# Two-layer graph network: layer 1's 17 coefficients in three column groups of the array in place of four

## The chip, the cores and the metric

The kernel runs on one core of a Trainium2 chip. The metric is the device time of one execution in microseconds (us). The core has a matrix engine (PE, with its weight loads shown apart as PEld), a vector engine (DVE), a scalar engine (ACT), GpSimd (POOL) and a queue that only issues transfers (SP). PE's clock is granted at one of two levels, 2.4 GHz (shown as 1.0) or 1.2 GHz (0.5).

## The reference, cut to what matters

```python
edge_index = jnp.stack([src, dst])                     # 200000 edges, sorted by dst; 12500 nodes of 32 features
h = jnp.maximum(_layernorm(x, axis=-1), 0.0)
x = x + _L0_gnn_ref(h, edge_index, edge_weight1, edge_attr_3, edge_attr_5, L0_gnn_W)
h = jnp.maximum(_layernorm(x, axis=-1), 0.0)
x = x + _L1_gnn_ref(h, ...)
# layer 1, per edge: x = h[src], y = h[dst], c = w_comp[etype] (16 numbers)
    msg = sum over b of c[b] * (x @ weight[b])          # 16 matrices of 32 x 32
    a = tanh(relu(sum(x_hat * y_hat) / sqrt(32)))       # x_hat, y_hat: linear in x, y and the edge type
    nei = segment_sum(a * msg, dst)
    curr = h[src of the node's last edge] @ self_loop_weight
    h_new = relu(nei + curr), 0 for nodes without edges
```

Layer 0 has the same shape, with 9 coefficients per edge and fixed combinations of small matrices.

## The kernel before, in words

The edges are cut into tiles of 128, twelve tiles to a group (J = 12), 131 groups for each layer. For a group, DVE writes Z: for every edge the layer's coefficients times a one-hot row over the 14 nodes that the tile can touch (WN = 14).
```python
def gather(g):
    wait(pool, L.summed, g.order() - 4)
```

Of the kernel before, what the change touches and what calls it, by code (L numbers as in the profile page):

```python
# [39 lines left out]
ACT = mybir.ActivationFunctionType  # L40
AX_X = mybir.AxisListType.X

N, F = 12500, 32
E = 200000
NREL, NBASE = 86, 16
P = 128
# [26 lines left out]
MQ = P // F  # L73
# [4 lines left out]
C0, C1 = 9, 17  # L78
PASSES = -(-N // WN)

QS = [[0, 3, 6, 9, 9], [0, 5, 9, 13, 17]]
CQ = [3, 5]
NQ = [3, 4]
NOWHERE = NWIN + 1
EPS = 1e-5

# [78 lines left out]
def wait(eng, sem, n):  # L165

    if not isinstance(n, int) or n > 0:
        eng.wait_ge(sem, n)
# [28 lines left out]
def build(nc, x, src_t, dst_t, dnext_t, dst, etype, edge, tile_first, tile_last, group_first, group_last, group_of_tile,  # L197
# [8 lines left out]
    with ExitStack() as ctx:  # L206
        def sb(name, shape, dt=F32):
            return ctx.enter_context(nc.sbuf_tensor(name, shape, dt))
# [28 lines left out]
        eps = sb("eps", [P, 1])  # L237
        cg_sb = sb("cg_sb", [P, CQ[0], F])
        w0_sb = sb("w0_sb", [P, CQ[0], F])
        w0c = sb("w0c", [P, CQ[0], 2 * F])  # L240
        w0_sum = sb("w0_sum", [P, CQ[0]])
        w1_sb = sb("w1_sb", [P, CQ[1], F])
        a1b_sb = sb("a1b_sb", [F, KA])
# [67 lines left out]
        flat = p_left[:].rearrange("p m k -> p (m k)")  # L311
        at = 2 * CQ[1] * HW
        G_sb = flat[:, 0:at].rearrange("p (c h w) -> p c h w", c=CQ[1], h=2)
# [279 lines left out]
        def _(pe):  # L593
# [29 lines left out]
            def edge_sums(n):  # L623
                L = layers[n]
                qs, cq = QS[n], CQ[n]
                no = OUT[n].stop - OUT[n].start
# [25 lines left out]
                def project(g):  # L652

                    hh, w = g.halves()

                    pe.wait_ge(L.G_set, g.order())
                    wait(pe, L.o_set, g.order() - 1)
                    wait(pe, L.added, g.order() - 1)
                    for h in range(hh):
                        for c in range(cq):  # L660
                            rows = NQ[n] * F
                            last = pe.matmul(o_ps[0:w, h, 0:no], G_sb[0:rows, c, h, 0:w], weights[0:rows, c, :],  # L662
                                             start=(c == 0), stop=(c == cq - 1))
                    last.then_inc(L.turned, 1)

                def project_in_quarters(g):

                    hh, w = g.halves()

                    pe.wait_ge(L.G_set, g.order())  # L670
                    wait(pe, L.oT_set, g.order() - 1)
                    wait(pe, L.added, g.order() - 1)
                    for c in range(cq):
                        rows, q = (P, c) if c < MQ else (F, 0)
                        last = pe.matmul(oT_ps[q * F:(q + 1) * F, 0:hh * w], weights[0:rows, c, :], G_sb[0:rows, c, 0:hh, 0:w],  # L675
                                         start=(c < MQ), stop=(c > 0), tile_position=(0, q * F))
                    last.then_inc(L.projected, 1)

                def sum_quarters(g):
# [10 lines left out]
                def place_rows(g):  # L690

                    hh, w = g.halves()

                    pe.wait_ge(L.o_set, g.order())
                    pe.wait_ge(L.R_set, g.order())
                    wait(pe, L.added, g.order() - 1)
                    pe.nop().then_inc(L.turn_go, 1)
                    for h in range(hh):
                        last = pe.matmul(win_ps[OUT[n]], o_sb[0:w, h, 0:no], R[0:w, g.b, h, :], start=(h == 0),  # L699
                                         stop=(h == hh - 1), tile_position=(0, OUT[n].start))  # L700
                    last.then_inc(L.placed, 1)

                def sum_edges(g, back):

                    wait(pe, L.G_set, g.order() - 1)
                    pe.wait_ge(L.gathered[g.q], g.gathers(n) * 16)
                    if not g.tail:
                        pe.wait_ge(L.picked, g.tiles_before(n, 1))
                    pe.wait_ge(L.Z_set, g.order() * 2 - 1)  # L710
                    for j in range(g.nj):
                        if j == JH:

                            pe.wait_ge(L.Z_set, g.order() * 2)
                        bank = G_ps[:, j // JH, 0:cq * HW].rearrange("p (c j n) -> p c j n", c=cq, j=JH)
                        for q in range(NQ[n]):
                            last = pe.matmul(bank[q * F:(q + 1) * F, 0:qs[q + 1] - qs[q], j % JH, :], xg[:, g.q, j, :],  # L717
                                             Z[:, g.b, j, qs[q] * WN:qs[q + 1] * WN], start=True, stop=True,
                                             tile_position=(0, q * F))
                        if j == g.nj - 1:  # L720
                            last.then_inc(L.summed, 1)
                        if back and j == min(g.nj, J // 3) - 1:
                            place_rows(back)

                def step(gs):
                    tiles = gs[0].found_tiles(n) if gs[0] else []
                    find_rows(tiles[0:1])
                    if n == 0 and gs[2]:
                        project(gs[2])
                    if n == 1 and gs[2]:  # L730
                        project_in_quarters(gs[2])
                    find_rows(tiles[1:])
                    if n == 1 and gs[2]:
                        sum_quarters(gs[2])
                    if n == 1 and gs[0]:
                        attention_rows(gs[0])
                    if gs[1]:
                        sum_edges(gs[1], gs[2])
                    elif gs[2]:
                        place_rows(gs[2])  # L740
# [49 lines left out]
        def _(act):  # L790
# [34 lines left out]
            def edge_copies(n):  # L825
                L = layers[n]
                cq = CQ[n]
# [42 lines left out]
                def copy_G(g):  # L870
                    hh, w = g.halves()

                    act.wait_ge(L.summed, g.order())
                    wait(act, L.turned, g.order() - 1)
                    bank = G_ps[:, 0:hh, 0:cq * HW].rearrange("p h (c w) -> p h c w", c=cq)
                    to = G_sb[:, 0:cq, 0:hh, 0:w].rearrange("p c h w -> p h c w")
                    if n == 1:
                        act.activation(to[0:F, :, cq - 1, :], bank[0:F, :, cq - 1, 0:w], ACT.Copy)  # L878
                    chunks, rows = min(cq, MQ), NQ[n] * F
                    act.activation(to[0:rows, :, 0:chunks, :], bank[0:rows, :, 0:chunks, 0:w], ACT.Copy).then_inc(L.G_set, 1)  # L880

                def copy_oT(g):
                    hh, w = g.halves()
# [11 lines left out]
                def step(gs):  # L895
                    if gs[2]:
                        copy_G(gs[2])
                    if n == 1 and gs[0]:
                        one_hots(gs[0])
                    if n == 1 and gs[2]:  # L900
                        copy_oT(gs[2])
                    if n == 1 and gs[1]:
                        attention(gs[1])
                    if n == 1 and gs[0]:
                        last_edges(gs[0])
                    if gs[1]:
                        placing(gs[1])
                    if gs[2]:
                        copy_o(gs[2])
# [439 lines left out]
def _quarters(w, layer):  # L1349
# [3 lines left out]
    for q in range(4):  # L1353
        lo, hi = QS[layer][q:q + 2]
        to[q, :, 0:hi - lo] = w[lo:hi].transpose(1, 0, 2)
# [58 lines left out]
```

## Time and profile before

| | |
|---|---|
| median of 3 runs | 4632.38 us (4622.65 to 4634.9) |
| the profiled execution | 4637.38 us |
| its span, first to last instruction | 4635.5 us |
| PE busy | 3578.4 us (77%) |
| DVE busy | 2689.9 us (58%) |
| POOL busy | 2301.7 us (50%) |
| ACT busy | 1097.0 us (24%) |
| mean granted clock of PE | 0.851 |

Layer 0 fills about the first 2130 us of the span, layer 1 runs from about 2220 us to the end. Busy time of PE counts matmuls by their recorded starts and modelled ends. Whether an engine sets the time is read from who waits for whom in a step, not from its share.

### The profile page before, as it was taken

To read this page: it belongs to the slowest core of one execution; us is meant where nothing else is said; L and a number is where in the kernel's file an instruction comes from. 1 tells how busy PE (TensorE), PEld (TensorE's weight loads), DVE (VectorE), ACT (ScalarE), POOL (GpSimd) and SP (SyncE) were. 2 spreads that over 40 slices of the span, in tenths; PEclk is the share of its full clock that TensorE was granted. 3 is DMA by queue.
4 is the path that set the end of the run, shared out by engine and by line. 5 is a ranking of instruction groups with operands and counts; after the bars stand their busy time and mean duration, and the time that the engine had idled before them with its cause. 6 is when DMAs were issued, how large, how long until landed. Compare 5 with 4: busy or idle time off the path is not lost.

```text
span 4635.5 us, 106735 instructions
## 1 busy us (share of the span) xinstructions
PE 3578.4 (77%) x41254; PEld 3052.1 (66%) x41254; DVE 2689.9 (58%) x3863; ACT 1097.0 (24%) x2563; POOL 2301.7 (50%) x2427
## 2 busy tenths in 40 slices
PE   3788888888888888885677777777777777777777
PEld 2677777777777777775566666666666666666666
DVE  5455555555555555555555665656656665556565
ACT  1111111111111111112233333333333333333332
POOL 5555555555555555553344444544444444445442
PEclk9889988888988989997788888888888888888887
DMA  3111111111111111111122222222222222222221
GB/s 102 21 21 20 20 21 19 20 20 21 20 20 21 20 20 21 21 20 54 35 38 39 38 37 38 40 37 37 37 41 37 38 39 38 37 37 39 39 37 35
DMA packets 216608, 150.09 MB, mean 32 GB/s; under 512 B 121048, under 2 KB 197261, under 8 KB 216079
## 3 DMA queue, kind: packets, MB, share of 16 engines
q0 software_dynamic: 77504, 39.84, 8.9%
q1 hardware_dynamic: 137999, 100.77, 8.8%
q8 instruction: 335, 5.49, 0.5%
q10 hardware_dynamic: 576, 2.40, 0.1%
q14 instruction: 194, 1.59, 0.1%
HBM read 134.58 MB, written 8.22 MB: 31 GB/s over the span
## 4 chain that ended last, share of the span: by engine, by line
PE 38%; issue 13%; another core or an unknown queue 2%; DVE 1%; ACT 1%; ACTq 0%; DVEq 0%
PE ps L636 20%; PE ps L717 7%; PE ps L649 5%; PE ps L675 2%; PE ps L699 1%; PE ps L687 1%; PE ps L599 0%; ACT p_left L846 0%; PE ps L619 0%; DVE room L1095 0%; DVE row_var L969 0%; ACT p_left L886 0%; DVE squares L996 0%; DVE H L966 0%
## 5 line engine op out<-in xcount | busy, mean ns | idle before, releaser
L564 POOL DMA_INDIRECT xg<-h_table,idx x2422 | 2290.8, 946 | 2272.7 <-PE ps L717 1530.1
L636 PE MATMUL ps<-h,blocks 128*128 128x448 f32 x9856 | 2284.3, 388 | 43.3 <-DVE blocks L1024 29.2
L636 PEld LDWEIGHTS ps<-h,blocks 128*128 128x128 f32 x9856 | 1937.9, 202 | 262.8 <-issue 76.6
L1024 DVE TENSOR_TENSOR blocks<-scratch,ps 128x896 fp32r<-128x896 int16 x704 | 761.2, 1082 | 882.8 <-remote 864.7
L717 PE MATMUL ps<-room,xg 128*32 128x42 f32 (+2 forms) x21882 | 699.4, 267 | 301.5 <-issue 297.4
L717 PEld LDWEIGHTS ps<-room,xg 128*32 128x32 f32 x21882 | 579.6, 144 | 429.0 <-issue 412.4
L1033 DVE SCALAR_TENSOR_TENSOR scratch<-ramp_sb,scratch,ps 128x448 f32<-128x448 f32 x704 | 476.4, 677 | 512.1 <-remote 250.7
L649 PE MATMUL ps<-att_tab,p_left 128*128 128x49 bf16 x4689 | 261.2, 200 | 555.3 <-issue 553.7
L1095 DVE TENSOR_TENSOR room<-coef,ps 128x756 f32<-128x756 f32 (+1 forms) x522 | 648.9, 1284 | 4.9 <-DVE ps L1044 0.2
L649 PEld LDWEIGHTS ps<-att_tab,p_left 128*128 128x128 bf16 x4689 | 201.6, 107 | 610.5 <-issue 609.5
L880 ACT ACTIVATE p_left<-ps 96x504 f32<-96x504 f32 (+2 forms) x262 | 168.8, 644 | 1200.8 <-PE ps L717 1200.7
L1038 DVE TENSOR_REDUCE xg<-scratch 128x32 f32<-128x448 f32 x704 | 436.6, 620 | 25.6
L893 ACT ACTIVATE p_left<-ps 84x128 f32<-84x128 f32 (+2 forms) x262 | 64.4, 246 | 1428.9 <-remote 1189.8
L846 ACT ACTIVATE p_left<-rows_b,node_all 128x512 bf16<-128x512 int16 x391 | 251.6, 705 | 48.8 <-PE ps L649 48.8
L699 PE MATMUL ps<-squares,p_left 84*64 84x128 f32 (+1 forms) x1044 | 241.3, 372 | 11.5 <-issue 10.6
L850 ACT ACTIVATE p_left<-p_left 128x1536 bf16<-128x1536 bf16 x131 | 193.5, 1477 | 4.1
L1076 DVE TENSOR_TENSOR coef<-ps,att 128x192 f32<-128x192 f32 x131 | 46.6, 356 | 232.8 <-issue 116.1
L865 ACT ACTIVATE squares<-ramp_sb,place 84x128 f32<-84x128 f32 x522 | 179.2, 391 | 9.7 <-issue 9.7
L1106 DVE TENSOR_TENSOR aggT<-aggT,ps 64x128 f32 (+1 forms) x262 | 74.1, 283 | 179.8 <-PE ps L699 137.2
L699 PEld LDWEIGHTS ps<-squares,p_left 84*64 84x64 f32 (+1 forms) x1044 | 144.4, 166 | 26.0 <-issue 13.0
L878 ACT ACTIVATE p_left<-ps 32x168 f32<-32x168 f32 x131 | 39.2, 300 | 476.9 <-PE ps L717 476.9
L662 PEld LDWEIGHTS ps<-w0c,p_left 96*84 96x84 f32 x1566 | 137.5, 155 | 11.3 <-ACT p_left L880 1.6
(108 smaller groups left out, 1144.5 us busy)
## 6 DMA issues: line engine op xcount, KB each, us to landing
xg<-h_table,idx POOLq DMA_INDIRECT x2422
rows_b<-typ_short SPq DMA_DIRECT2D x130, 258.0 KB
scratch<-q_short SPq DMA_DIRECT2D x260, 96.0 KB
rows_b<-dst_short SPq DMA_DIRECT2D x130, 126.0 KB
coef<-in_edge_dram SPq DMA_DIRECT2D x130, 54.0 KB
att_tab<-p_table SPq DMA_DIRECT2D x393, 8.1 KB
p_table<-room SPq DMA_DIRECT2D x8, 297.0 KB
X<-in_x_dram SPq DMA_DIRECT2D x7, 224.0 KB, 4.3
```

Source lines behind the costliest of these rows:

```text
L564: pool.indirect_dma_start(xg[:, g.q, t - g.s * J, :], None, h_table[n], bass.IndirectOffsetOnAxis(ap=idx[:, t:t + 1], axis=0)).then_inc(L. ...
L636: last = pe.matmul(found_ps[b], blocks[:, b, c, :], h_2[:, a, c], start=(c == 0 and a == 0), stop=(c == NCH - 1 and a == 1))
L649: last = pe.matmul(to, one_hot[:, j, :], att_tab[:, g.b, j // JS, a, :], start=(a == 0), stop=(a == 2))
L699: last = pe.matmul(win_ps[OUT[n]], o_sb[0:w, h, 0:no], R[0:w, g.b, h, :], start=(h == 0), stop=(h == hh - 1), tile_position=(0, OUT[n].start))
L717: last = pe.matmul(bank[q * F:(q + 1) * F, 0:qs[q + 1] - qs[q], j % JH, :], xg[:, g.q, j, :], Z[:, g.b, j, qs[q] * WN:qs[q + 1] * WN], sta ...
L846: act.activation(one_hot[:, js, :].rearrange("p j e -> p (j e)"), rows_b[:, b, js.start * P:js.stop * P], ACT.Abs, bias=node, scale=-1.0). ...
L850: act.activation(one, one, ACT.Relu, bias=1.0, scale=-1.0).then_inc(L.one_hot_set, 1)
L865: act.activation(R[0:w, g.b, h, :], iota_row[0:w, :], ACT.Abs, bias=at, scale=-1.0)\
L1024: dve.tensor_tensor(blocks[:, b], q_b[:, g.b, i, :].unsqueeze(1).broadcast_to([P, NCH, P]), block_ps.unsqueeze(2).broadcast_to([P, NCH, P] ...
L1033: dve.scalar_tensor_tensor(out=picked, in0=iota_row[:, 0:MC].unsqueeze(1).broadcast_to([P, F, MC]), scalar=place_in_block[:, bass.ds(u, 1) ...
L1038: dve.tensor_reduce(xg[:, g.q, j, :], picked, AX_X, ALU.add).then_inc(L.picked, 1)
L1095: dve.tensor_tensor(Z[:, b, js, 0:C * WN].rearrange("p j (c n) -> p j c n", n=WN), coef[:, js, :].unsqueeze(3).broadcast_to([P, k, C, WN]) ...
```

## The change

Layer 1's coefficients are cut 6, 6, 5 (84, 84 and 70 columns) in place of 5, 4, 4, 4. `sum_edges` issues three matmuls per tile, 36 per group in place of 48. The bank holds six coefficients side by side in place of five, so the sums are projected in six chunks: five of 96 rows and one of 64. ACT's two copies become one of 64 partitions and one of 96 partitions with five chunks. Projection chunk c goes to column group c % 4. Z, the attention rows, the gathers and layer 0 are as before.

```diff
-QS = [[0, 3, 6, 9, 9], [0, 5, 9, 13, 17]]
-CQ = [3, 5]
-NQ = [3, 4]
+QS = [[0, 3, 6, 9, 9], [0, 6, 12, 17, 17]]
+CQ = [3, 6]
+NQ = 3
+CHUNK = [[3 * F, 3 * F, 3 * F], [3 * F, 3 * F, 3 * F, 3 * F, 3 * F, 2 * F]]
...
                     for c in range(cq):
-                        rows, q = (P, c) if c < MQ else (F, 0)
+                        rows, q = CHUNK[n][c], c % MQ
                         last = pe.matmul(oT_ps[q * F:(q + 1) * F, 0:hh * w], weights[0:rows, c, :], G_sb[0:rows, c, 0:hh, 0:w],
-                                         start=(c < MQ), stop=(c > 0), tile_position=(0, q * F))
+                                         start=(c < MQ), stop=(c + MQ >= cq), tile_position=(0, q * F))
...
-                        for q in range(NQ[n]):
+                        for q in range(NQ):
                             last = pe.matmul(bank[q * F:(q + 1) * F, 0:qs[q + 1] - qs[q], j % JH, :], xg[:, g.q, j, :],
...
-                    if n == 1:
-                        act.activation(to[0:F, :, cq - 1, :], bank[0:F, :, cq - 1, 0:w], ACT.Copy)
-                    chunks, rows = min(cq, MQ), NQ[n] * F
-                    act.activation(to[0:rows, :, 0:chunks, :], bank[0:rows, :, 0:chunks, 0:w], ACT.Copy).then_inc(L.G_set, 1)
+                    whole = CHUNK[n].count(NQ * F)
+                    if whole < cq:
+                        rows = CHUNK[n][whole]
+                        act.activation(to[0:rows, :, whole, :], bank[0:rows, :, whole, 0:w], ACT.Copy)
+                    rows = NQ * F
+                    act.activation(to[0:rows, :, 0:whole, :], bank[0:rows, :, 0:whole, 0:w], ACT.Copy).then_inc(L.G_set, 1)
```

```order
L636 MATMUL ps<-h_2,blocks 128x448 x14
L675 MATMUL ps<-p_left,w1_sb 32x168 x5
L632 REGISTER_ALU
L636 MATMUL ps<-h_2,blocks 128x448 x14
L687 MATMUL ps<-four_units,p_left 84x32 x2
L643 REGISTER_ALU
L644 ISA
L649 MATMUL ps<-att_tab,p_left 128x49 x36
L710 ISA
L717 MATMUL ps<-room,xg 32x5x14
L717 MATMUL ps<-room,xg 32x4x14 x3
```

Of the change, the same engine and place:

```order
L637 MATMUL ps<-h_2,blocks 128x448 x14
L676 MATMUL ps<-p_left,w1_sb 32x168 x6
L633 REGISTER_ALU
L637 MATMUL ps<-h_2,blocks 128x448 x14
L688 MATMUL ps<-four_units,p_left 84x32 x2
L644 REGISTER_ALU
L645 ISA
L650 MATMUL ps<-att_tab,p_left 128x49 x36
L711 ISA
L718 MATMUL ps<-room,xg 32x6x14 x2
L718 MATMUL ps<-room,xg 32x5x14
```

No instruction has moved against another: a tile's four matmuls (one of 5 x 14 columns, three of 4 x 14) have become three (two of 6 x 14, one of 5 x 14), four tiles still stand ahead of place_rows and eight behind it, and the projection has six matmuls in place of five. On ACT, the copies of the sums in the same step, before:

```order
L878 ACTIVATE p_left<-ps 32x168
L880 ACTIVATE p_left<-ps 128x2x4x84
L846 ACTIVATE p_left<-rows_b,node_all 128x512 x3
L850 ACTIVATE p_left<-p_left 128x1536
L886 ACTIVATE p_left<-ps 128x168
```

And of the change:

```order
L881 ACTIVATE p_left<-ps 64x168
L883 ACTIVATE p_left<-ps 96x2x5x84
L847 ACTIVATE p_left<-rows_b,node_all 128x512 x3
L851 ACTIVATE p_left<-p_left 128x1536
L889 ACTIVATE p_left<-ps 128x168
```

The second copy moves 840 elements per partition in place of 672, and nothing else on ACT differs.

## Rows read from the trace of the kernel before

**Rows 1.** Waits in layer 1, 2300 to 4600 us: total us, times, longest.

```profile
POOL xg L564 <- PE ps L717: 840.7, 121, 7.9
ACT p_left L893 <- remote: 781.2, 123, 9.2
PE ps L649 <- issue: 535.6, 531, 2.7
```

**Rows 2.** Timeline of POOL: start, us, instruction, and the idle time before it.

```profile
3308.05 0.94 POOL L564 DMA_INDIRECT xg<-h_table,idx  x1 [0.30 <-issue]
3316.30 0.94 POOL L564 DMA_INDIRECT xg<-h_table,idx  x1 [7.31 <-PE ps L717]
...
3326.28 0.94 POOL L564 DMA_INDIRECT xg<-h_table,idx  x1 [0.30 <-issue]
3334.22 0.94 POOL L564 DMA_INDIRECT xg<-h_table,idx  x1 [7.01 <-PE ps L717]
```

**Rows 3.** Timeline of PE over the same two steps.

```profile
3305.31 0.54 PE L649 MATMUL ps<-att_tab,p_left 128*128 128x49 bf16 x15 [0.28 <-issue]
3308.45 0.20 PE L649 MATMUL ps<-att_tab,p_left 128*128 128x49 bf16 x1 [2.60 <-issue]
...
3311.28 0.96 PE L649 MATMUL ps<-att_tab,p_left 128*128 128x49 bf16 x19 [0.51 <-issue]
3312.18 1.02 PE L717 MATMUL ps<-room,xg 128*32 128x70 f32 x31
3312.94 0.42 PE L699 MATMUL ps<-squares,p_left 84*32 84x128 f32 x1
...
3313.15 0.42 PE L699 MATMUL ps<-squares,p_left 84*32 84x128 f32 x1
...
3313.79 1.70 PE L717 MATMUL ps<-room,xg 128*32 128x56 f32 x54
3315.42 3.51 PE L636 MATMUL ps<-h,blocks 128*128 128x448 f32 x14
3318.86 0.89 PE L675 MATMUL ps<-p_left,w_sb 128*32 128x168 f32 x10
3319.68 5.94 PE L636 MATMUL ps<-h,blocks 128*128 128x448 f32 x28
...
3325.72 0.21 PE L649 MATMUL ps<-att_tab,p_left 128*128 128x49 bf16 x2
...
3329.13 1.05 PE L649 MATMUL ps<-att_tab,p_left 128*128 128x49 bf16 x32 [0.54 <-issue]
...
3333.35 3.11 PE L636 MATMUL ps<-h,blocks 128*128 128x448 f32 x14
```

**Rows 4.** Timeline of ACT in the first of these steps.

```profile
3304.12 0.31 ACT L886 ACTIVATE p_left<-ps 128x168 f32<-128x168 f32 x1 [3.79 <-remote]
...
3311.45 0.22 ACT L893 ACTIVATE p_left<-ps 84x64 f32<-84x64 f32 x1 [5.46 <-remote]
3315.63 0.30 ACT L878 ACTIVATE p_left<-ps 32x168 f32<-32x168 f32 x1 [3.96 <-PE ps L717]
3315.83 0.71 ACT L880 ACTIVATE p_left<-ps 128x672 f32<-128x672 f32 x1
```

**Rows 5.** Stretches: busy us of PE, PEld, DVE, ACT, POOL; PEclk; DMA share; GB/s.

```profile
3312.20:3315.40 3.20, 3.20 (x102) 2.99 (x100) 1.78 (x4) 0.00 (x0) 0.00 (x0) 0.50 0.05 8
3315.40:3316.00 0.60, 0.60 (x5) 0.54 (x3) 0.60 (x2) 0.37 (x2) 0.00 (x0) 0.50 0.04 14
...
3333.30:3333.90 0.60, 0.60 (x6) 0.52 (x4) 0.60 (x2) 0.42 (x2) 0.00 (x0) 1.00 0.11 27
```

**Rows 6.** Timeline of PE at layer 0's edge sums (42 columns), two groups.

```profile
1510.71 1.34 PE L717 MATMUL ps<-room,xg 128*32 128x42 f32 x48
...
1526.58 0.80 PE L717 MATMUL ps<-room,xg 128*32 128x42 f32 x48
```

**Rows 7.** The same two as stretches, columns as in rows 5.

```profile
1510.71:1511.90 1.19, 1.19 (x49) 1.17 (x48) 1.16 (x3) 0.00 (x0) 0.00 (x0) 0.50 0.00 0
1526.58:1527.50 0.92, 0.80 (x49) 0.68 (x48) 0.89 (x3) 0.06 (x1) 0.00 (x0) 1.00 0.00 0
```

More of the change, by code:

```diff
@@ L660, in project @@
                         for c in range(cq):
-                            rows = NQ[n] * F
+                            rows = CHUNK[n][c]
                             last = pe.matmul(o_ps[0:w, h, 0:no], G_sb[0:rows, c, h, 0:w], weights[0:rows, c, :],
```

## The prediction

> **What bounds the kernel now.** Only layer 1 changes, so I read a steady pair of its steps. I began with the waits, because PE's 77% busy share does not say whether a shorter or longer PE stage is seen in the time. [rows 1] say two things at once. POOL waits for the edge sums 121 times, 840.7 us in all: some 7 us in every step. And PE itself stands still inside L649, 535.6 us in all, with nothing in the profile that it would wait for.
>
> The timelines put these together. POOL's burst of gathers begins 0.9 us after the sums end: PE goes on to L636 at 3315.42 and the first gather starts at 3316.30, after 7.31 us of idle. The burst of nine is over at 3326.28 + 0.94 = 3327.22 [rows 2]. PE runs ahead into L649, stands, and resumes at 3329.13, 1.9 us after the burst [rows 3]. In the step before, the burst ends at 3308.05 + 0.94 = 3308.99 and PE resumes at 3311.28, 2.3 us after it. So PE's progress between the sums and the resumption follows POOL's burst and not PE's own work: the second step has 42 matmuls at L636, the first 28, and the second still resumes sooner after its sums, since its burst has one gather less. ACT shows that PE is behind what its records say: it waits 3.79 us for the projection at L675 and 5.46 us for L687, both long since recorded [rows 4]. Why PE is held while the gathers run, these rows do not tell. I take the hold as a fact of this kernel.
>
> The loop of a step is then: end of the sums, POOL's burst, about 2 us, the rest of L649, the sums again. Check: from 3315.42 to 3333.35 is 17.93 us [rows 3]; 0.88 to the burst, 10.92 of burst, 1.91 to resume, 0.98 + 3.24 for the rest of L649 and the sums. **What stands between the resumption and the end of the sums is paid in full; what stands in the hold is free as long as it stays shorter than the hold.**
>
> **The edge sums, the term that decides.** From the first L717 at 3312.18 to L636 at 3315.42 are 3.24 us [rows 3], at a granted clock of 0.50 [rows 5], the 1.2 GHz level. What does this time consist of? The place_rows records of 128 columns, all in one column group of the array, start 0.213 us apart (3312.94, 3313.15, and the fourth ends at 3313.79): 1.67 ns per column of a record, two cycles of 1.2 GHz. If all column groups shared one stream, the 64 records after 3313.79 would need 64 x 56 x 1.67 ns = 6.0 us and more; they take 1.63. So the four column groups stream side by side, each at 1.67 ns per column, and the widest chain of one group is what counts. That is the third group, since place_rows is in it too:
> - eight records of 56 columns before place_rows: 8 x 56 x 1.67 = 0.75 us (row: 3312.18 to 3312.94, 0.76),
> - place_rows: 4 x 0.213 = 0.85 us,
> - sixteen after it: 16 x 56 x 1.67 = 1.49 us, and 0.14 to the next record (row: 1.63).
>
> The first group, 24 x 70 x 1.67 = 2.80 us, hides behind these 3.09. Layer 0 confirms the price: eight tiles of 42 columns are 16 x 42 x 1.67 = 1.12 us at clock 0.50 and half of it at 1.00; the rows have 1.34 and 0.80, in which the last record's own length (about 0.2) is counted [rows 6, 7].
>
> After the change the third group has 70 columns: 8 x 70 x 1.67 + 0.85 + 16 x 70 x 1.67 = 3.65 us, and the first two need 24 x 84 x 1.67 = 3.36, still hidden. The sums grow by 24 x 14 x 1.67 = **0.56 us at the low clock, 0.28 at the high one**. The 12 matmuls fewer per group give nothing back, since they ran beside the others. Which clock does the added stretch get? It lies just behind where the sums ended; there the clock is 0.50 in one step and 1.00 in the next [rows 5]. I take the middle, 0.42 us. Times 131 groups: +55 us; the ends are 131 x 0.28 = +37 and 131 x 0.56 = +73.
>
> In its section on instruction overhead, the page TensorEngine Tiling (Array Packing) of the Trainium skill says the opposite of this price: every matmul carries about 60 cycles of overhead, so that one of few columns costs as much as one of 60. By it 84 columns would hardly cost more than 56 or 70, and a quarter fewer matmuls would be a gain. The place_rows records of 0.213 us each, in a stage whose other records average 0.025, speak for columns and not for a number of instructions. The price by that rule is the first rival below.
>
> **Fewer attention matmuls done in the hold.** PE runs ahead a certain number of matmuls and then stands: from the end of the sums to the first halt, 14 + 10 + 28 + 4 + 2 = 58 records in the second step (four are L687's), and 14 + 10 + 14 + 4 + 15 = 57 in the first, whose 42 ahead of L649 follow from the program's order [rows 3]. The count is the same though the mix is not. The sixth projection chunk adds two records ahead of L649, so two of L649's move behind the resumption. They cost there (0.96 - 0.2) / 18 = 0.042 us each at the low clock, (1.05 - 0.2) / 31 = 0.027 at the high one: 0.05 to 0.08 us per step, 0.07 taken, x 131 = **+9 us**. If the halt does not depend on a count, it is nothing.
>
> **Edits costed at nothing.** The projection itself: its 0.82 us (3318.86 to 3319.68) stand in the hold, which has 5.4 us of standing still in the first step and 3 in the second. The two chunks of the second column group become as long as the first group's two, not longer. If the cover were gone, a chunk's two records of 168 columns would be 0.14 to 0.56 us. ACT's copies: 0.30 + 0.71 us; the second goes from 672 to 840 elements, at (0.71 - 0.30) / 504 per element about +0.14 us. The projection is issued 3.4 us after the sums' end and the copies end 1.1 us after it, so 2.3 us of L636 hide this [rows 3, 4]; without cover it would be 131 x 0.14 = 18 us. Of the queues, none is passed: SP and POOL issue what they did, in the same order. Z is the same, and DVE's work with it.
>
> **Sum.** 4637.4 (the profiled execution) + 55 + 9 = 4701. That execution is 5 us above the median of the runs, so the forecast is 4632.4 + 64 = 4696, and I say 4697.
>
> **The rivals.**
> - *A matmul costs by its instruction, not by its columns* (faster). 3.24 us for 96 + 4 records is 0.032 each; 24 fewer give 0.78 us per step: 4632 - 102 + 9 = about 4540. The 0.213 us of a place_rows record speak against it. 4%.
> - *The hold is not released by POOL's burst but works off PE's instructions* (faster). With 96 - 72 - 2 = 22 fewer of some 190 records in a step, a hold proportional to them would shrink by 12% of its 13.7 us, 1.6 us per step: 4632 - 210 + 55 = about 4480. A part of it, 0.49 us per step, would already cancel the loss. It decides if steps no longer keep their 1.9 to 2.3 us behind the burst. That 28 and 42 matmuls at L636 both end with the burst speaks against it. 5%.
> - *The longer sums are absorbed* (no change): POOL's burst would have to be able to start before this step's sums end. The xg buffers are four deep, but the 7.31 us wait on L717 in every step says that they are used up. Then 4632 to 4641. 5%.
> - *The wider groups are not hidden behind place_rows* (slower still): if the first two groups, at 84 columns, cannot run ahead while the third does place_rows, the sums take 3.36 + 0.85 + 0.14 = 4.35 us, +1.1 at the low clock: 131 x 0.84 at the mixed clock = +110, about 4750. Their distance to the third, 14 columns, is what it was, which speaks against it. 5%.
>
> The page TensorE: Matmul & The Clock Gate of the Trainium skill, in its section on packing small matmuls, has packed column tiles last as long as one matmul of theirs and some nanoseconds per tile more. By that too, the widest tile sets the time.
>
> **How the numbers follow.** My forecast, 0.28 to 0.56 us per group with 0 to 0.08 behind the hold, spans 4632 + 37 = 4669 to 4632 + 84 = 4716 and has 81%. The range is widened to 4665 and 4735 for a partial loss of cover. The base varies by 12 us between runs. What a measurement of this kernel can tell from no change is about 0.3%, 14 us. Slower by more than that: 81 + 5, and a little of the second rival that only shrinks the loss, 87%; within it 5%; faster 8%.
>
> **What would show it.** The edge sums: third-group records about 0.117 us apart at the low clock, and a stage of 3.8 us where it was 3.24, with place_rows unchanged. POOL's wait for L717 longer by 0.5 us per step, its bursts and the 1.9 to 2.3 us behind them unchanged. L649 resuming with two more matmuls to go. Layer 0 to the microsecond as before. Wrong, if the stage is shorter than before, if the time between the sums' end and PE's resumption changes by more than 0.2 us, or if the period of a step does not grow by what the sums grow.

## The result

| | before | after |
|---|---|---|
| median | 4632.35 us (4622.65 to 4634.9, 4 runs) | 4698.34 us (4694.37 to 4711.84, 4 runs) |
| ratio | | 1.0152, 95% interval 1.0126 to 1.0177 |
| span of the profiled execution | 4635.5 us | 4694.1 us |
| mean granted clock of PE | 0.851 | 0.856 |

The change makes this kernel 1.5% slower. The forecast was 4697 us.

The waits of the kernel after, in layer 1 (2300 to 4660 us), that answer to [rows 1], and PE's in front of sum_quarters (L688):

```profile
POOL xg L565 <- PE ps L718: 903.9, 121, 8.4
...
PE ps L650 <- issue: 458.5, 447, 2.7
...
PE ps L688 <- issue: 73.9, 32, 6.4
PE ps L688 <- ACT p_left L889: 35.0, 19, 5.4
```

POOL waits for the sums 63 us longer in the same 121 places, 0.52 us a time. PE stands 77 us less inside L650 and 68 us more in front of sum_quarters (109 us), where the kernel before has 41.3 us (the last numbers of its row in a list of all groups of instructions, 2300 to 4600 us):

```profile
L687 PE MATMUL ps<-four_units,p_left 128*84 128x32 f32 x504 | 54.8, 231 | 41.3 <-issue 29.2 <-ACT p_left L886 11.1
```

In the timeline of POOL, where [rows 2] have bursts of nine or ten gathers and 7.3 us between them, little else has changed:

```profile
3312.19 0.95 POOL L565 DMA_INDIRECT xg<-h_table,idx  x1 [0.30 <-issue]
3320.44 0.94 POOL L565 DMA_INDIRECT xg<-h_table,idx  x1 [7.30 <-PE ps L718]
...
3331.68 0.94 POOL L565 DMA_INDIRECT xg<-h_table,idx  x1 [0.30 <-issue]
3340.09 0.94 POOL L565 DMA_INDIRECT xg<-h_table,idx  x1 [7.47 <-PE ps L718]
```

PE over the same steps, the answer to [rows 3]:

```profile
3315.03 1.01 PE L650 MATMUL ps<-att_tab,p_left 128*128 128x49 bf16 x33 [0.55 <-issue]
3315.97 1.20 PE L718 MATMUL ps<-room,xg 128*32 128x84 f32 x22
3316.92 0.42 PE L700 MATMUL ps<-squares,p_left 84*32 84x128 f32 x1
...
3317.77 1.88 PE L718 MATMUL ps<-room,xg 128*32 128x70 f32 x40
3319.58 3.11 PE L637 MATMUL ps<-h,blocks 128*128 128x448 f32 x14
3322.62 1.16 PE L676 MATMUL ps<-p_left,w_sb 96*32 96x168 f32 x12
3323.71 3.12 PE L637 MATMUL ps<-h,blocks 128*128 128x448 f32 x14
...
3334.66 0.85 PE L650 MATMUL ps<-att_tab,p_left 128*128 128x49 bf16 x16 [0.50 <-issue]
3335.43 1.19 PE L718 MATMUL ps<-room,xg 128*32 128x84 f32 x22
3336.38 0.42 PE L700 MATMUL ps<-squares,p_left 84*32 84x128 f32 x1
...
3337.24 2.07 PE L718 MATMUL ps<-room,xg 128*32 128x70 f32 x40
3339.24 2.94 PE L637 MATMUL ps<-h,blocks 128*128 128x448 f32 x12
```

The second pair of sums, 3335.43 to 3339.24, takes 3.81 us where [rows 3] have 3.24: +0.57. Ahead of place_rows stand 0.95 us (0.76 before), place_rows is 0.86 as before, and behind it are 2.00 (1.63 before). The bursts end at 3313.14 and 3332.62, PE resumes at 3315.03 and 3334.66: 1.9 and 2.0 us behind them (1.9 and 2.3 in [rows 2] and [rows 3]; on average over the steps 2.0 us with three found tiles and 2.2 with two, in both kernels). The granted clock of both sums and of what follows the first, as stretches (columns as in [rows 5]):

```profile
3315.97:3319.58 3.61, 3.61 (x79) 3.44 (x76) 2.88 (x6) 0.00 (x0) 0.00 (x0) 0.54 0.08 18
3335.43:3339.24 3.81, 3.81 (x79) 3.53 (x77) 2.30 (x5) 0.00 (x0) 0.00 (x0) 0.50 0.05 9
3319.58:3320.20 0.62, 0.62 (x5) 0.59 (x4) 0.59 (x2) 0.51 (x2) 0.00 (x0) 1.00 0.02 1
```

The first sums end just after the clock has risen, and are 0.2 us shorter for it. Such a mixture of 0.56 and 0.28 is what the prediction took at its middle.

### The profile page after: what moved, and what is told of

Read it like the earlier page. It is cut to its first block, busy times and chain, and to the rows that moved or that the text cites. A ratio compares the mean times of both kernels' runs of the same rounds, so it can differ in the third digit from the quotient of the medians.

```text
span 4694.1 us, 101007 instructions
## 1 busy us (share of the span) xinstructions
PE 3649.2 (78%) x38390; PEld 3125.2 (67%) x38390; DVE 2689.4 (57%) x3863; ACT 1116.5 (24%) x2563; POOL 2301.8 (49%) x2427
## 4 chain that ended last, share of the span: by engine, by line
PE 37%; issue 13%; another core or an unknown queue 3%; ACT 1%; DVE 1%; ACTq 0%; DVEq 0%
PE ps L637 18%; PE ps L718 8%; PE ps L650 5%; PE ps L676 3%; PE ps L700 1%; PE ps L688 1%; ACT p_left L847 1%; PE ps L600 1%; PE ps L620 0%; ACT p_left L889 0%; DVE room L1098 0%; ACT p_left L883 0%; DVE row_var L972 0%; DVE squares L999 0%
## 5 line engine op out<-in xcount | busy, mean ns | idle before, releaser
L637 PE MATMUL ps<-h,blocks 128*128 128x448 f32 x9856 | 2273.6, 387 | 43.6 <-issue 21.7
L637 PEld LDWEIGHTS ps<-h,blocks 128*128 128x128 f32 x9856 | 1926.9, 200 | 266.2 <-issue 71.8
L718 PE MATMUL ps<-room,xg 128*32 128x42 f32 (+2 forms) x18756 | 748.8, 275 | 298.8 <-issue 294.6
L718 PEld LDWEIGHTS ps<-room,xg 128*32 128x32 f32 x18756 | 631.2, 145 | 420.3 <-issue 405.4
L650 PE MATMUL ps<-att_tab,p_left 128*128 128x49 bf16 x4689 | 256.2, 205 | 477.6 <-issue 476.8
L650 PEld LDWEIGHTS ps<-att_tab,p_left 128*128 128x128 bf16 x4689 | 206.0, 110 | 523.1 <-issue 521.6
L883 ACT ACTIVATE p_left<-ps 96x504 f32<-96x504 f32 (+2 forms) x262 | 187.9, 717 | 1206.1 <-PE ps L718 1206.0
L1041 DVE TENSOR_REDUCE xg<-scratch 128x32 f32<-128x448 f32 x704 | 436.5, 620 | 25.6
L881 ACT ACTIVATE p_left<-ps 64x168 f32<-64x168 f32 x131 | 39.7, 303 | 539.4 <-PE ps L718 539.4
L676 PE MATMUL ps<-p_left,w_sb 96*32 96x168 f32 (+1 forms) x1572 | 152.0, 316 | 2.9 <-ACT p_left L883 2.3
```

The lines of the kernel that those rows point to most:

```text
L637: last = pe.matmul(found_ps[b], blocks[:, b, c, :], h_2[:, a, c], start=(c == 0 and a == 0), stop=(c == NCH - 1 and a == 1))
L650: last = pe.matmul(to, one_hot[:, j, :], att_tab[:, g.b, j // JS, a, :], start=(a == 0), stop=(a == 2))
L1041: dve.tensor_reduce(xg[:, g.q, j, :], picked, AX_X, ALU.add).then_inc(L.picked, 1)
```

## The experiments

One thing has to be said ahead of them. The experiments ran on several chips, and the kernel before took 4554 us on two of them (e1 to e4; e5c, e6b, e7) and 3153 us on two others (e5, e5b, e6, e3b, c1); the change was first timed where it took 4632. On the 3153 us chips no trace shows PE standing inside its attention matmuls. That is called "without the hold" below, and the standing that the prediction found "the hold". Everything was run on one chip at a time, so what belongs to the chip and what to the hour can't be told apart; "chip" stands for both. Each ratio below is to the kernel before on the same chip.

**e1: place_rows in the fourth column group, which has no sums.**

```diff
-SUMS0, CENTRED0, SUMS1 = (slice(a * F, (a + 1) * F) for a in range(3))
+SUMS0, CENTRED0, _, SUMS1 = (slice(a * F, (a + 1) * F) for a in range(4))
...
-        win_ps = ps[0:3 * F, 4, 2 * HW + 4 * F:2 * HW + 4 * F + P]
+        win_ps = ps[:, 4, 2 * HW + 4 * F:2 * HW + 4 * F + P]
...
-        aggT = sb("aggT", [3 * F, NWIN])
+        aggT = sb("aggT", [P, NWIN])
```

> The changed kernel (6, 6, 5), with the window rows of layer 1 at partitions 96 to 127, so that place_rows runs in the fourth column group, which has no sums, and not in the third. My theory, the longest chain of one column group sets the edge sums: the third group falls to 24 x 70 columns, the first two stay at 24 x 84, so the chain goes from 3.65 to 3.36 us at the low clock, 0.29 us less (0.15 at the high one): about 4698 - 131 x 0.21 = 4670 us. Rival, only the widest tile counts and place_rows lies beside it already, or stops all groups wherever it runs: no change, 4698. Rival, the time follows the number of instructions: no change, 4698.

Measured: 4623.82 us, 1.0158 (1.014 to 1.0177) of before. The change itself was not run on this chip; the nearest kernel is e7 below, 1.0159 on one of the same speed. The expected gain of 0.6% is not there. At the low clock the sums themselves did as the theory says. In this timeline of PE they run from 3315.46 to 3318.97, 3.51 us at the low clock in place of 3.81:

```profile
3315.46 0.92 PE L718 MATMUL ps<-room,xg 128*32 128x84 f32 x15
...
3316.72 2.31 PE L718 MATMUL ps<-room,xg 128*32 128x84 f32 x43
3318.97 3.14 PE L637 MATMUL ps<-h,blocks 128*128 128x448 f32 x14
```

Counted over all steps of layer 1, first to last record of the sums, they take 3.21 and 2.60 us (steps with two and with three found tiles), in e7 3.40 and 2.68. So only 0.20 and 0.08 us are won, where 0.29 and 0.15 were priced; the clock over the sums is 0.50 and 0.64, in e7 0.53 and 0.69, so the shorter stage has less of the high clock. That would still be 18 us. But POOL's first gather comes 0.12 us later behind the last record in e1's steps of the second kind (1.15 us, in e7 1.03), and PE's next sums 0.2 us later, so these steps are not shorter at all; why is open. The time of e1 does not decide for the chain theory. Its stage at the low clock does: 3.36 + 0.14 us were priced and 3.51 measured, and place_rows cannot have stopped the other groups, which would have given 4.35.

**e2: the third group as wide as the others.**

```diff
+FIRST = [[0, 3, 6], [0, 6, 11]]
+WIDE = [3, 6]
-CHUNK = [[3 * F, 3 * F, 3 * F], [3 * F, 3 * F, 3 * F, 3 * F, 3 * F, 2 * F]]
+CHUNK = [[3 * F, 3 * F, 3 * F], [3 * F] * 6]
...
-                            last = pe.matmul(bank[q * F:(q + 1) * F, 0:qs[q + 1] - qs[q], j % JH, :], xg[:, g.q, j, :],
-                                             Z[:, g.b, j, qs[q] * WN:qs[q + 1] * WN], start=True, stop=True,
+                            last = pe.matmul(bank[q * F:(q + 1) * F, 0:WIDE[n], j % JH, :], xg[:, g.q, j, :],
+                                             Z[:, g.b, j, FIRST[n][q] * WN:(FIRST[n][q] + WIDE[n]) * WN], start=True, stop=True,
```

The weights of layer 1 are laid out to match, with zero for the doubled coefficient.

> The changed kernel with the third group six coefficients wide too (coefficient 11 is summed twice, the second time with weight zero): 84, 84, 84 columns, and the same 36 matmuls and six chunks. The widest group is as wide as before, only the group that also does place_rows has grown. My theory: its chain grows by 24 x 14 x 1.67 ns = 0.56 us at the low clock, 0.28 at the high one, 4698 + 131 x 0.42 = about 4753 us. Rival, the widest group sets the time: no change, 4698. Rival, instructions count: no change.

Measured: 4669.48 us, 1.0249 (1.0232 to 1.0266) of before. Against e7's 1.0159 (all six chunks on 96 rows there too) that is 0.9% for 14 more columns in a group that was the narrowest, with no matmul more; 1.2% were expected. Both rivals said none. Counted over all steps the sums take 3.79 and 3.21 us, in e7 3.40 and 2.68. And on the same chip e1, whose widest group is 84 columns too, is 46 us faster. The timeline of PE, one group's sums at the low clock, from 3310.62 to 3314.66, 4.04 us:

```profile
3310.62 1.34 PE L720 MATMUL ps<-room,xg 128*32 128x84 f32 x24
3311.76 0.42 PE L702 MATMUL ps<-squares,p_left 84*32 84x128 f32 x1
...
3312.61 2.12 PE L720 MATMUL ps<-room,xg 128*32 128x84 f32 x40
3314.66 3.15 PE L639 MATMUL ps<-h,blocks 128*128 128x448 f32 x14
```

The chain's price for this row is 8 x 84 x 1.67 + 0.85 = 1.97 us to the end of place_rows (row: 1.99) and 2.24 behind it, where the row has 2.05: there the clock rose again before the end (0.60 on average over 3312.61 to 3314.66).

**e3: 5, 5, 5 and 2 coefficients, with place_rows in the narrow fourth group.** The kernel before with e1's three lines, and

```diff
-QS = [[0, 3, 6, 9, 9], [0, 5, 9, 13, 17]]
+QS = [[0, 3, 6, 9, 9], [0, 5, 10, 15, 17]]
...
-                        rows, q = (P, c) if c < MQ else (F, 0)
+                        rows, q = (P if c < 2 else 3 * F, c % MQ) if n else (P, c)
...
-                        act.activation(to[0:F, :, cq - 1, :], bank[0:F, :, cq - 1, 0:w], ACT.Copy)
-                    chunks, rows = min(cq, MQ), NQ[n] * F
+                        act.activation(to[0:3 * F, :, 2:cq, :], bank[0:3 * F, :, 2:cq, 0:w], ACT.Copy)
+                    chunks, rows = (2, P) if n == 1 else (cq, 3 * F)
```

> The kernel before with four column groups of 5, 5, 5 and 2 coefficients and place_rows in the fourth, narrow one; 48 matmuls per group and five projection chunks as before. My theory: the chains are 24 x 70 x 1.67 = 2.80 us for the first three and 24 x 28 x 1.67 + 0.85 = 1.97 for the fourth, so 2.80 in place of 3.09 at the low clock, 0.29 less (0.15 at the high one): 4632 - 131 x 0.21 = about 4604 us, faster than both kernels. Rival, the widest group sets the time (70 columns before too): no change, 4632. Rival, the time follows the number of instructions: no change, 4632.

Measured: 4533.23 us, 0.9952 (0.9938 to 0.9966) of before, where 0.994 was expected. A group's sums run from 3313.51 to 3316.52, 3.01 us where [rows 3] have 3.24, with the same 48 matmuls and a first group as wide as before:

```profile
3313.51 0.92 PE L717 MATMUL ps<-room,xg 128*32 128x70 f32 x26
3314.13 0.40 PE L699 MATMUL ps<-squares,p_left 84*32 84x128 f32 x1
...
3314.80 1.79 PE L717 MATMUL ps<-room,xg 128*32 128x70 f32 x55
3316.52 3.58 PE L636 MATMUL ps<-h,blocks 128*128 128x448 f32 x14
```

**e4: four idle matmuls more in the projection.**

```diff
+        no_w = sb("no_w", [P, F])
...
                         last = pe.matmul(oT_ps[q * F:(q + 1) * F, 0:hh * w], weights[0:rows, c, :], G_sb[0:rows, c, 0:hh, 0:w],
-                                         start=(c < MQ), stop=(c > 0), tile_position=(0, q * F))
+                                         start=(c < MQ), stop=False, tile_position=(0, q * F))
+                    for q in range(MQ):
+                        last = pe.matmul(oT_ps[q * F:(q + 1) * F, 0:hh * w], no_w[:], G_sb[:, 0, 0:hh, 0:w],
+                                         start=False, stop=True, tile_position=(0, q * F))
...
+            dve.memset(no_w[:], 0.0)
```

> The kernel before with four more matmuls in the projection, with zero weights, one in each column group: eight more records ahead of the attention rows, inside the hold, and nothing else. If PE runs ahead a fixed number of matmuls and then stands until POOL's burst is over, eight fewer attention matmuls are done in the hold and cost 0.027 to 0.042 us each behind it: +0.28 us per step, 4632 + 36 = about 4668 us (and my +9 us for the two records of the change holds). If what stands in the hold is free altogether: 4632.

Measured: 4614.88 us, 1.0117 (1.0098 to 1.0135) of before, +53 us by the ratio where 36 were expected. So matmuls added inside the hold are not free. But the way is not the expected one alone. A step with two found tiles, PE's timeline and ACT's copy of the projection (L890):

```profile
3315.31 0.89 PE L676 MATMUL ps<-p_left,w_sb 128*32 128x168 f32 x10
3316.13 0.49 PE L679 MATMUL ps<-p_left,no_w 128*32 128x168 f32 x8
3316.55 3.15 PE L637 MATMUL ps<-h,blocks 128*128 128x448 f32 x14
3325.01 0.74 PE L691 MATMUL ps<-four_units,p_left 128*84 128x32 f32 x4 [5.30 <-issue]
3325.75 0.74 PE L650 MATMUL ps<-att_tab,p_left 128*128 128x49 bf16 x14
3327.39 1.08 PE L650 MATMUL ps<-att_tab,p_left 128*128 128x49 bf16 x22 [0.89 <-issue]
```

```profile
3324.55 0.31 ACT L890 ACTIVATE p_left<-ps 128x168 f32<-128x168 f32 x1 [8.04 <-remote]
```

PE already stands in front of sum_quarters (L691), so that all 36 attention matmuls come late. And there it waits for ACT: L691 starts 0.15 us after ACT's copy ends, and that copy starts only 7.9 us after the last record of L679. So it is with every halt at sum_quarters (a start over 0.55 us after the record before). In e4 there are 95 of them in layer 1, in the kernel before 35, and each ends some 0.14 us after ACT's copy. From the projection's last record to ACT's copy the median is 5.8 us in e4 and 2.3 before. By count over the steps, the last halt leaves 25.6 and 33.9 records ahead of the sums, in the kernel before (on its own chip) 16.6 and 31.0: nine and three more, where eight were expected in both. So a limit on the number of matmuls and a projection signal that is itself held until later would both give a loss, and e4 does not tell them apart.

**e5: nine gathers and three found tiles in every group of layer 1.**

```diff
-NP = [[2 if s < 8 else 3 for s in range(FULL)], [2 if s < 8 else 3 if s == FULL - 1 else 3 - s % 2 for s in range(FULL)]]
+NP = [[2 if s < 8 else 3 for s in range(FULL)], [2 if s < 8 else 3 for s in range(FULL)]]
```

> The kernel before with three found tiles and nine gathers in every group of layer 1 from the ninth on (as layer 0 has them), in place of two and three by turns. PE has 14 more matmuls at L636 in every second step, POOL one gather less. If the hold ends with POOL's burst: every step resumes 14.0 us after the sums, as the steps with nine gathers do, and the others give up 1.25 us of gather: 61 x 1.2 = 4632 - 75 = about 4557 us. If the hold is PE's own work, or a backlog of its instructions: 61 x 14 more matmuls of 0.22 us and more, 4632 + 188 = 4820 us or so.

It fell on a 3153 us chip: 3300.79 us, 1.0469 (1.0452 to 1.0487). Repeated as e5b (1.0462 of 3152.76, again such a chip) and as e5c:

> As e5 (nine gathers and three found tiles in every group), which so far ran without the hold only. With it: 0.984 of before if the hold is POOL's burst, about 1.04 if it is PE's own work. Without it: 1.046 as measured.

With the hold: 4499.86 us, 0.9875 (0.9848 to 0.9903). 61 steps with 14 more matmuls at L636 each, and the kernel is faster, since POOL's burst is one gather shorter. Without the hold the same edit costs 147 us, and in the trace of e5 POOL waits 238.6 us for PE's sums (1700 to 3280 us). The two signs tell the two mechanisms apart: with the hold the time follows POOL's burst, without it PE's work shows.

**e6: three gathers fewer in each full group of layer 1.** POOL's work is cut, and with it the transfers that it starts; PE, DVE and ACT do all they did:

```diff
-        return self.nj if self.tail else J - NP[n][self.of_loop()]
+        return self.nj if self.tail else J - 3 * n - NP[n][self.of_loop()]
```

and the same `3 * n` in the two counts that the waits use. The kernel leaves the rows of these tiles as an earlier group left them, so its result is not the reference's.

> The kernel before with three gathers fewer in every full group of layer 1 (their rows keep what an earlier group left, so the sums of those tiles are of other rows): POOL's burst is 3.75 us shorter, and PE, DVE and ACT do all they did. If the hold lasts as long as POOL's burst: 122 steps lose up to 3.75 us, less where PE's own work of 7 to 10 us becomes the limit, a ratio to before of about 0.90 to 0.93 on a chip with the hold. If the hold comes from PE's or the queue SP's own work: no change. On a chip without the hold: no change, since POOL waits for PE there too.

The first run was on a 3153 us chip: 3140.49 us, 0.9958 (0.9942 to 0.9975). No change was expected, since POOL would wait for PE there too; this was wrong, as c1 below shows, and 12 us are won. e6b had a chip with the hold:

> As e6 (three gathers fewer in each full group of layer 1, whose tiles keep other rows), in the hope of a chip with the hold, since the first run fell on one without it. With the hold: steps shorter by up to 3.75 us, 0.90 to 0.93 of before if the hold is POOL's burst; 1.00 if it is not. Without it: 0.996 as measured.

3993.94 us, 0.8759 (0.8727 to 0.8792), more than the expected 0.90 to 0.93: 560 us gone by taking work from an engine that was busy for half of the time. POOL's and PE's timelines of one of its steps with three found tiles, whose burst has six gathers:

```profile
3308.13 0.95 POOL L564 DMA_INDIRECT xg<-h_table,idx  x1 [6.11 <-PE ps L717]
...
3314.39 0.95 POOL L564 DMA_INDIRECT xg<-h_table,idx  x1 [0.30 <-issue]
```

```profile
3317.14 1.09 PE L649 MATMUL ps<-att_tab,p_left 128*128 128x49 bf16 x36
3318.16 0.61 PE L717 MATMUL ps<-room,xg 128*32 128x70 f32 x31
...
3319.91 3.10 PE L636 MATMUL ps<-h,blocks 128*128 128x448 f32 x14
```

The burst is over at 3315.34, before PE comes to L649. All 36 attention matmuls run through, the clock has not fallen (1.00 over 3307.30 to 3319.90), and the sums take 1.75 us. Its other steps, with seven gathers, still stand inside L649. The gain, 4.6 us for each of 122 steps, is larger than the 3.75 us of three gathers. A part of the rest is the clock: in the steps with six gathers it is 1.00 over the sums, which take 1.73 us on average, where the kernel before (on its own chip) has 0.60 and 2.68. That the clock is all of it was not shown. Nor does e6b tell POOL's issuing of gathers from the transfers themselves as what holds PE.

**c1: the change once more, on a chip without the hold.**

> The changed kernel once more, since the kernel before took 4632, 4554 and 3153 us on three chips: on the third PE is never held while POOL gathers. On a chip with the hold: 1.013 to 1.016 of before, as measured, from 131 x 0.42 us of longer sums. On a chip without it PE's own work fills the step and the clock is the high one: the sums grow by 131 x 0.28 = 37 us and the sixth chunk adds two records of PE, about +45 us of 3153, a ratio of 1.014. Rival, without the hold the wider groups hide under something or the fewer instructions pay: a ratio of 1.00 or less.

Measured: 3158.87 us, 1.0017 (1.0008 to 1.0027) of before's 3152.76. The expected 1.4% is missing. A pair of its steps is, in PE's timeline:

```profile
2502.66 3.10 PE L637 MATMUL ps<-h,blocks 128*128 128x448 f32 x14
2505.70 1.16 PE L676 MATMUL ps<-p_left,w_sb 96*32 96x168 f32 x12
...
2515.89 3.11 PE L637 MATMUL ps<-h,blocks 128*128 128x448 f32 x14
...
2526.28 3.10 PE L637 MATMUL ps<-h,blocks 128*128 128x448 f32 x14
```

13.23 + 10.39 = 23.62 us, with PE busy all of it. POOL meanwhile issues 19 gathers at one per 1.25 us, 23.7 us, without a pause, and its waits for the sums come to 6.7 us in layer 1, 1700 to 3130 us:

```profile
POOL xg L565 <- issue: 338.5, 1111, 0.3
...
POOL xg L565 <- PE ps L718: 6.7, 22, 0.3
```

So in c1 both PE and POOL are full. The kernel before was not profiled on such a chip. The nearest is e3b below, on the same chip and as fast as before: POOL pauses there as little (0.9 us of waits for the sums), while PE waits in the same stretch for what DVE makes:

```profile
PE ps L636 <- DVE blocks L1024: 20.1, 23, 1.9
...
PE ps L717 <- DVE room L1095: 17.5, 50, 1.2
```

In c1 neither wait is among the rows. So the added time of PE, at the high clock 0.27 us in the sums and 0.27 in the projection of each step, filled time in which PE would have waited. By these rows POOL's gathers set the pace in both kernels, though for the kernel before this is an inference from its neighbour. DVE's work stands close behind them, since taking three gathers away (e6) wins only 12 us.

**e3b: 5, 5, 5, 2 without the hold.**

> As e3 (5, 5, 5 and 2 coefficients, place_rows in the fourth group). With the hold a ratio of 0.995 to before, as measured. Without it, at the high clock: 131 x 0.15 = 19 us less of 3153, 0.994. Rival, the widest group alone sets the time: 1.000.

3151.82 us, 0.9996 (0.9987 to 1.0006): no change, and so not the 0.994 expected without the hold. The cause is that of c1: PE's sums are not what its step waits for there.

**e7: the change with the sixth chunk on 96 rows.** Its last 32 rows are zero.

```diff
-                        rows, q = CHUNK[n][c], c % MQ
+                        rows, q = 3 * F, c % MQ
...
                 split_p(u)
+            dve.memset(G_sb[2 * F:3 * F, 5], 0.0)
```

> The changed kernel with the sixth projection chunk on 96 rows like the other five (rows 64 to 95 are zero, written once). In the third-group-of-six kernel, whose chunks all have 96 rows, the projection takes 0.69 us, with the 64-row chunk 1.09 (0.82 before). On a chip with the hold the projection is hidden: the same 1.015 of before. On a chip without it PE's step gets 0.4 us back where it does not wait for the vector engine: 0.994 to 1.000 of before, in place of 1.0017. Rival, the 64-row chunk costs nothing: 1.015 or 1.0017 again.

With the hold: 4626.42 us, 1.0159 (1.0131 to 1.0187), the ratio of the change. From the projection's first record to the next L637 are 0.69 us (3306.68 to 3307.37) in place of 1.09 (3322.62 to 3323.71 in the kernel after):

```profile
3306.68 0.76 PE L676 MATMUL ps<-p_left,w_sb 96*32 96x168 f32 x12
3307.37 3.10 PE L637 MATMUL ps<-h,blocks 128*128 128x448 f32 x14
```

A projection shorter by 0.4 us, 51 us over 128 steps if it were paid, changes nothing that the interval would show: it lies in the hold. It was not run where there is none, and so what it was expected to give back there stays untested.

## Why the prediction was right

**What bounds the kernel.** The loop of sums, burst, about 2 us and the rest of L649 stood the tests made for it. Fewer gathers shorten the kernel by 12% (e6b), one gather less and 14 matmuls more in every second step shorten it by 1.2% (e5c), and in the kernel after the 1.9 to 2.0 us behind the burst have stayed. Counted over the steps of layer 1, PE resumes 15.4 and 14.0 us after the last record of the sums (steps with two and with three found tiles), as before. The rival that had the hold work off PE's instructions is out: 22 fewer records per step did not shorten it. Why PE is held while gathers run, and why only on some chips, is open.

**The edge sums.** Counted over all steps, first to last record, the sums take 3.44 and 3.01 us on average, before 2.92 and 2.68: +0.51 and +0.33, on average 0.42 us, the value taken. 131 x 0.42 is the 55 us of the sum. The price of 0.56 and 0.28 us was worked out; that the middle fits to 0.01 us is partly luck, since it came from the clock behind one step of each kind. One reading was wrong and harmless: 54 records and not 64 are left at 3313.79 [rows 3]. The program has 32 ahead of place_rows, but 42 have started by then. The kernel after has 40 left of 72, with 24 ahead in the program. So the other groups ran ahead while the third did place_rows, which is what the chain theory needs. e2 and the parts of the row at 3335.43 confirm that it is the chain of the third group with place_rows in it, and not the widest group or the number of matmuls. The rival in which place_rows stops the other groups (4750 us, a stage of 4.35) is refused by the 3.81 us. The rival in which a matmul costs by its instruction is refused too: with 12 matmuls (24 records) fewer the stage is longer by 15 to 18%. The rule that the prediction took from the page TensorEngine Tiling (Array Packing) of the Trainium skill, section Instruction Overhead, is that a matmul of one column takes as long as one of 60. That rule is not tested by these runs: a record of 56 columns takes 56 x 1.67 = 93 ns of its group, 112 cycles of the 1.2 GHz clock, well above 60. So it does not say, as the prediction read it, that 84 columns would hardly cost more than 56.

**The attention matmuls behind the hold.** +9 us were given. By the count over the steps the sums begin 0.06 and 0.14 us later after the last sums' end than before, 0.1 x 128 = 12 us, and the last halt leaves 18.6 and 31.9 records ahead of them, before 16.6 and 31.0. The size is right, the mechanism is not shown. The prediction counted 57 records to the first halt in its first step, but PE had already stood there 1.66 us in front of sum_quarters, after 38 records:

```profile
3304.57 0.46 PE L687 MATMUL ps<-four_units,p_left 128*84 128x32 f32 x4 [1.66 <-issue]
```

Half of the steps with two found tiles halt there first, and each time PE goes on 0.14 us after ACT's copy of the projection ends. After the change there are 53 such halts in layer 1, before 35. A later signal of the projection would thus move attention matmuls behind the hold without any limit on their number, and e4 leaves both open. In e4 the loss is also larger than the count of added matmuls gives.

**The edits costed at nothing.** The projection was said to get no longer. It did: 1.09 us from its first record to the next L637, before 0.82 [rows 3]. The 64-row chunk is the cause, since with all six on 96 rows it is 0.69 (e7). This step of the prediction was wrong. Its own 0.27 us cost nothing, because the hold covered them, as was said: with e7's 0.69 us the ratio is the same. ACT's second copy took 0.86 us in this step (0.71 before, +0.14 expected), also under cover:

```profile
3319.90 0.86 ACT L883 ACTIVATE p_left<-ps 96x840 f32<-96x840 f32 x1
```

**The sum.** From the first sums of layer 1 to its last the trace has 2434 us, before 2367: +67, as 55 + 12. Layer 0's steps were shorter in this execution (15.82 against 15.88 us, 122 steps), together some 7 us, and the spans differ by 58.6. Layer 0's program is the same, so these 7 us are no effect of the change; their cause is open. The medians differ by 66 us. That 4697 was said and 4698 measured is luck at this precision, since the runs of the kernel after lie 17 us apart. And the prediction did not have that all of this holds only where PE is held. Elsewhere it would have been wrong by nearly the whole effect: 6 us in place of 65 (c1).

## What to carry to other kernels

Column groups of the array stream side by side, so the price of a stage is the longest chain of one group, with everything that another stage puts into that group: widen the groups that have room and keep the one with the extra work narrow (where PE is held, 5, 5, 5, 2 with place_rows in the last is 0.5% faster than the kernel before, three groups in place of four 1.5% slower). Before costing a step of an engine, find what it resumes behind: here a burst of gathers on another engine decided which microseconds of PE were free. And run an edit on more than one chip before believing its size, since the same edit was worth 1.5% on one and 0.2% on another.

## What the runs showed that was not expected

- The kernel before takes 4632, 4554 or 3153 us, by the chip. From the projection's last record to ACT's copy of it the median is 0.2 us on a 3153 us chip (c1), with the hold 2.3 us before and 2.7 after. PE's mean clock is 0.98 to 0.99 there, in place of 0.85 to 0.87 (0.89 in e5c and 0.92 in e6b, where the hold is shorter).
- With the hold PE moves in steps of 0.70 us: inside L649 of the kernel before, matmuls that come after a halt start mostly 0.7, 1.4, 2.1 or 2.8 us after the one before, at either clock.
- In steps with three found tiles PE's first halt comes 57 to 60 matmuls after the end of the sums in 53 of 61 steps of the kernel before.
- A last chunk of other height than 96 or 128 rows lengthens the projection: 0.82 us with one of 32 rows, 1.09 with one of 64, 0.69 with none (e7, e3), to the next matmul at the high clock.
- A stage made shorter where the clock is about to rise can win less than its columns (e1: 0.20 and 0.08 us of 0.29 and 0.15). The clock over the shorter sums was lower by 0.03 and 0.05.
